# Moving the query preparation of the next tile behind the head loop, and two int8 steps from VectorE to GpSimd, in a two-layer attention/FFN kernel

## The reference, cut to what matters

```python
# x: (8, 4096, 1024) float32, one batch element per core
x = x + ln(attn(ln(x), gamma0, w_qkv0, w_out0))     # layer 0, attention
x = x + ln(int8_ffn(ln(x), rhs))                    # layer 0, FFN with absmax int8
x = x + ln(attn(ln(x), gamma1, w_qkv1, w_out1))     # layer 1, attention
x = x + ln(qlora_ffn(ln(x), ...))                   # layer 1, six 4-bit linears with LoRA

# attn: 8 heads of 128, causal; l2-normalised rows, qkv, softmax(q k^T) v, out projection
# int8_ffn: s = max(|x|)/127 per row; q = round(x/s); (q @ q_rhs) * s * s_rhs
```

## Time and profile before

| | us |
|---|---|
| median of 3 runs | 8509.21 |
| lowest and highest | 8452.44, 8510.84 |
| the profiled execution | 8492.97 |
| its span, first to last instruction (core 1) | 8491.4 |
| TensorE busy | 4956.7 (58%) |
| VectorE busy | 2899.7 (34%) |
| ScalarE busy | 3002.4 (35%) |
| GpSimd busy | 481.8 (6%) |
| mean granted TensorE clock | 0.764 of full |

### The profile page before, as it was taken

How to read it: one execution, slowest core, us unless ns; L and a number is a source line. 1 busy time by engine, 2 the same in 40 slices (tenths; PEclk the granted TensorE clock), 3 DMA queues, 4 the chain that set the end, 5 groups by cost and what they waited for, 6 DMA issues and landing times.

```text
span 8491.4 us, 56576 instructions; the slowest of 8 cores (8444.4 to 8491.4 us)
## 1 busy us (share of the span) xinstructions
PE 4956.7 (58%) x18624; PEld 1752.6 (21%) x18624; DVE 2899.7 (34%) x4937; ACT 3002.4 (35%) x4569; POOL 481.8 (6%) x612
## 2 busy tenths in 40 slices
PE   4644566677679333366455667677780566667553
PEld 1221111122122111122111122222220222222121
DVE  4443322221221566444333221221213433433445
ACT  1212334344457121122123344445551243333332
POOL 0001000000000000000000000000002101100000
PEclk8766778788789666666667788788895787778776
DMA  2021101000100121300211100000004201110111
GB/s 75 30 65 44 36 28 35 33 29 19 33 25 9 63 89 72 109 30 30 66 40 40 36 29 23 33 29 18 25 19 140 70 1 41 41 33 13 52 47 57
DMA packets 120312, 362.13 MB, mean 43 GB/s; under 512 B 24464, under 2 KB 24464, under 8 KB 120016
## 3 DMA queue, kind: packets, MB, share of 16 engines
q1 hardware_dynamic: 120016, 358.51, 13.0%
HBM read 291.07 MB, written 67.37 MB: 42 GB/s over the span
## 4 chain that ended last, share of the span: by engine, by line
PE 50%; DVE 22%; DMA 14%; ACT 8%; issue 3%; POOL 2%; SPq 1%; DVEq 0%; ACTq 0%
PE pf L813 8%; PE pf L853 8%; PE pf L1136 8%; PE pf L842 7%; DMA xq<-xbuf 4%; PE pf L638 3%; PE pf L912 3%; ACT probs L823 3%; DVE rcp_row L864 3%; PE pf L664 3%; PE pf L742 2%; DMA xq<-x 2%; PE pb L481 2%; POOL probs L831 2%; DMA xbuf<-xq 2%
## 5 line engine op out<-in xcount | busy, mean ns | idle before, releaser
L823 ACT ACTIVATE probs<-pf,negM_col 128x512 bf16<-128x512 f32 x2304 | 1582.8, 687 | 1495.9 <-PE pf L813 1480.6
L481 PE MATMUL pb<-ident_bf,prep_bf 128*128 128x128 bf16 x1536 | 198.6, 311 | 1710.2 <-DVE prep_bf L723 705.6
L842 PE MATMUL pf<-probs,v_sb 128*128 128x512 bf16 x2304 | 946.4, 411 | 415.2 <-ACT probs L823 236.5
L864 DVE RECIPROCAL rcp_row<-pf 1x512 f32<-1x512 f32 x128 | 428.3, 3346 | 2005.2 <-PE pf L853 2004.7
L813 PE MATMUL pf<-qT,kT 128*128 128x512 bf16 x2304 | 951.4, 422 | 16.3 <-ACT qT L747 16.3
L853 PE MATMUL pf<-probs,ones_col 128*1 128x512 bf16 x2304 | 915.3, 397 | 0.0
L831 POOL TENSOR_SCALAR_AFFINE_SELECT probs<-probs 128x512 bf16<-128x512 bf16 x512 | 313.4, 612 | 6006.6 <-ACT probs L823 6006.6
L481 PEld LDWEIGHTS pb<-ident_bf,prep_bf 128*128 128x128 bf16 x1536 | 148.0, 141 | 1768.0 <-DVE prep_bf L723 725.5
L1148 ACT ACTIVATE ySB<-pf,bcol 128x512 bf16<-128x512 f32 x384 | 263.8, 687 | 694.4 <-PE pf L1140 690.5
L540 ACT ACTIVATE sq<-pb 128x1024 bf16<-128x1024 bf16 x128 | 131.0, 1023 | 913.1 <-DVE cols L534 913.1
L1136 PE MATMUL pf<-hT,wbuf 128*128 128x512 bf16 x1536 | 386.3, 397 | 50.2 <-ACT ySB L1148 47.5
(11 more groups left out here) (134 smaller groups left out, 5346.3 us busy)
## 6 DMA issues: line engine op xcount, KB each, us to landing
xq<-xbuf SPq DMA_DIRECT2D x128, 512.0 KB, 3.5
xbuf<-xq SPq DMA_DIRECT2D x96, 512.0 KB, 2.6
xq<-x SPq DMA_DIRECT2D x64, 512.0 KB, 4.6
rcp_bc<-rowrt SPq DMA_DIRECT2D x128, 256.0 KB, 3.7
xq4f<-xbuf SPq DMA_DIRECT2D x64, 512.0 KB, 4.0
wstage<-wqkvT SPq DMA_DIRECT2D x48, 512.0 KB, 4.4
wstage_i<-qwT SPq DMA_DIRECT2D x48, 512.0 KB, 3.7
screp<-scT SPq DMA_DIRECT2D x384, 64.0 KB, 2.3
```

What stands on the lines that cost most here:

```text
L481: v = p.add("tensor", lambda e, j=j: e.transpose(M.pb[pslot][:, j, :], M.prep_bf[:, prep_slot, j * 128:(j + 1) * 128], M.ident_bf[:]), wai ...
L823: ev = p.add("scalar", lambda e, kc=kc, h=h, ps=ps: e.activation(M.probs[:, kc % 2, :], ps[:], AF.Exp, bias=M.negM_col[:, h:h + 1], scale= ...
L842: p.add("tensor", lambda e, h=h, kc=kc, pO=pO: e.matmul(pO[:], M.v_sb[:, kc, h * 128:(h + 1) * 128], M.probs[:, kc % 2, :], start=(kc == 0 ...
L864: rc = p.add("vector", lambda e, pR=pR: e.reciprocal(M.rcp_row[:], pR[0:1, :]), waits=rw, inc="ve")
```

## The change

Two parts. In attention, `q_prep_tile` and `q_mm_group` go back into `q_prep` and `q_mm`. The head loop holds no preparation. After the last head the four row tiles are prepared, then the out projection runs, then all eight groups of Q, then `bound_prep` and the epilogue as before. In the int8 FFN, scaling and rounding go to GpSimd, in place in one of two buffers (`apply_scr`, `scrF2`), and the two casts, the transposes and the copy of row tile i are emitted by `_quant_fin` after the normalisation and the scale steps of row tile i+1. The casts wait for GpSimd.

```diff
@@ emit_prologue_group, mode "quant"
+    qpend = []
+    def _quant_fin(t, i, rne, B):
+        p.add("vector", lambda e, B=B: e.tensor_copy(M.scrI[:], B[:]),
+              waits=[("ge", rne)], inc="ve")
+        ps_ = i % 2
+        gw2 = [p.prep_gate[ps_]] if p.prep_gate[ps_] else []
+        vap = p.add("vector", lambda e, ps_=ps_: e.tensor_copy(
+            M.prep_bf[:, ps_, :], M.scrI[:]), waits=gw2, inc="ve")
+        consume(t, i, ("ve", vap), i % 2)
...
+            B = (M.apply_scr, M.scrF2)[i % 2]
...
-            zv = p.add("vector", lambda e, t=t: e.tensor_scalar(
-                M.apply_scr[:], M.apply_scr[:], cf[:, t, 2:3], None, ALU.mult),
-            p.add("vector", lambda e: e.tensor_scalar(
-                M.apply_scr[:], M.apply_scr[:], MAGIC, -MAGIC, ALU.add, ALU.add),
-                inc="ve")
-            p.add("vector", lambda e: e.tensor_copy(M.scrI[:], M.apply_scr[:]),
-                  inc="ve")
+            p.add("gpsimd", lambda e, t=t, B=B: e.tensor_scalar(
+                B[:], B[:], cf[:, t, 2:3], None, ALU.mult),
+                waits=[("ve", cv)], inc="ge")
+            rne = p.add("gpsimd", lambda e, B=B: e.tensor_scalar(
+                B[:], B[:], MAGIC, -MAGIC, ALU.add, ALU.add), inc="ge")
+            p.f0chain_gate[i % 2] = ("ge", rne)
+            qpend.append((t, i, rne, B))
+            if len(qpend) > 1:
+                _quant_fin(*qpend.pop(0))
+    while qpend:
+        _quant_fin(*qpend.pop(0))
@@ emit_attn, end of the head loop
-            if qt + 1 < nq:
-                if h == 0:
-                    qp_evs = []
-                if h < 4:
-                    q_prep_tile(qt + 1, h, qp_evs)
-                    if h == 3:
-                        xnT_ready = ("ve", max(qp_evs))
-                else:
-                    qev_n = q_mm_group(h - 5, xnT_ready) if h >= 5 else None
         attnout_ready = ("ve", p.c("ve"))
-        p.feat8_gate = None
+        if qt + 1 < nq:
+            xnT_ready = q_prep(qt + 1)
@@ after the out projection
         if qt + 1 < nq:
-            for fo in range(3, H):
-                qev_n = q_mm_group(fo, xnT_ready)
-            p.xnT_free[0] = p.add("scalar", _nop, inc="nf0")
-            qT_ready = ("ae", qev_n)
+            qT_ready = q_mm(qt + 1, xnT_ready)
             negM_evs = bound_prep(qt + 1, qT_ready)
```

More of the change, by code:

```diff
@@ L60, in __init__ @@
         self.rows_gate = []
-        self.f0chain_gate = None
+        self.f0chain_gate = [None, None]
         self.negMb_gate = [None] * 8
@@ L349, in emit_prologue_group @@
             p.xq_free[bufs[i][2]] = p.c(bufs[i][2])
+            consume(t, i, ("ve", vap), i % 2)
         else:
+            B = (M.apply_scr, M.scrF2)[i % 2]
             p.add("vector", lambda e, t=t, sve=sve: e.reciprocal(cf[:, t, 1:2], sve),
                   waits=[("ae", sq)], inc="ve")
-            aw2 = [p.f0chain_gate] if p.f0chain_gate else []
-            p.add("vector", lambda e, t=t, xsl=xs[i]: e.tensor_scalar(
-                M.apply_scr[:], xsl, cf[:, t, 0:1], cf[:, t, 1:2], ALU.add,
+            aw2 = [p.f0chain_gate[i % 2]] if p.f0chain_gate[i % 2] else []
@@ L356, in emit_prologue_group @@
+            p.add("vector", lambda e, t=t, xsl=xs[i], B=B: e.tensor_scalar(
+                B[:], xsl, cf[:, t, 0:1], cf[:, t, 1:2], ALU.add,
                 ALU.mult), waits=aw2, inc=["ve", bufs[i][2]])
             p.xq_free[bufs[i][2]] = p.c(bufs[i][2])
-            p.add("vector", lambda e: e.tensor_reduce(
-                col(M, 8), M.apply_scr[:], AX.X, ALU.max,
+            p.add("vector", lambda e, B=B, i=i: e.tensor_reduce(
+                col(M, 8 + i % 2), B[:], AX.X, ALU.max,
                 apply_absolute_value=True), inc="ve")
-            p.add("vector", lambda e: e.tensor_scalar(col(M, 9), col(M, 8), 1e-12,
-                                                      1.0 / 127.0, ALU.max,
-                                                      ALU.mult), inc="ve")
@@ L364, in emit_prologue_group @@
-            p.add("vector", lambda e, t=t: e.reciprocal(cf[:, t, 2:3], col(M, 9)),
-                  inc="ve")
[L366 to L369, removed]
-            zv = p.add("vector", lambda e, t=t: e.tensor_scalar(
-                M.apply_scr[:], M.apply_scr[:], cf[:, t, 2:3], None, ALU.mult),
-                inc="ve")
@@ L382, in emit_prologue_group @@
-        consume(t, i, ("ve", vap), i % 2)
+            p.add("vector", lambda e, i=i: e.tensor_scalar(
+                col(M, 10 + i % 2), col(M, 8 + i % 2), 1e-12,
+                1.0 / 127.0, ALU.max, ALU.mult), inc="ve")
+            p.add("vector", lambda e, t=t, i=i: e.reciprocal(
+                cf[:, t, 2:3], col(M, 10 + i % 2)), inc="ve")
+            p.add("vector", lambda e, t=t, i=i: e.tensor_mul(
+                col(M, 12 + i % 2), cf[:, t, 2:3], cf[:, t, 2:3]), inc="ve")
+            cv = p.add("vector", lambda e, t=t, i=i: e.tensor_scalar(
+                cf[:, t, 3:4], col(M, 12 + i % 2), 1e-5, None, ALU.mult),
+                inc="ve")
@@ L383, in emit_prologue_group @@
+    if mode == "quant":
+        return None
     return None
@@ L705, in emit_attn, with q_prep @@
     nq = min(NQ, LIMIT_BQ)
-    def q_prep_tile(qt, tt, evs):
-        for tt in (tt,):
+    def q_prep(qt):
+        evs = []
+        for tt in range(4):
             t = qt * 4 + tt
@@ L728, in q_prep_tile @@
             evs.append(emit_prep_to_xnT(p, M, tt, 0, tp))
[L730 to L733, removed]
         return ("ve", max(evs))
[L736 to L750, removed]
     def q_mm(qt, xnT_ready):
         for fo in range(H):
-            qev = q_mm_group(fo, xnT_ready)
+            pfk = M.pf[fo % 2]
+            w0 = [xnT_ready, wq_ready]
+            if p.pf_gate[fo % 2]:
+                w0.append(p.pf_gate[fo % 2])
+            for fi in range(NF):
+                mv = p.add("tensor", lambda e, fo=fo, fi=fi, pfk=pfk: e.matmul(
+                    pfk[:], M.wbuf1[:, fi, fo * 128:(fo + 1) * 128],
+                    M.xnT[:, 0, fi, :], start=(fi == 0), stop=(fi == NF - 1)),
+                    waits=(w0 if fi == 0 else ()),
+                    inc=("mm" if fi == NF - 1 else None))
+            qev = p.add("scalar", lambda e, fo=fo, pfk=pfk: e.activation(
+                M.qT[:, fo, :], pfk[:], AF.Copy), waits=[("mm", mv)], inc="ae")
+            p.pf_gate[fo % 2] = ("ae", qev)
         p.xnT_free[0] = p.add("scalar", _nop, inc="nf0")
@@ L893, in emit_attn @@
             p.pO_gate[hp] = ("ve", nv)
-            if qt + 1 < nq:
-                if h == 0:
-                    qp_evs = []
-                if h < 4:
-                    q_prep_tile(qt + 1, h, qp_evs)
-                    if h == 3:
-                        xnT_ready = ("ve", max(qp_evs))
-                else:
-                    qev_n = q_mm_group(h - 5, xnT_ready) if h >= 5 else None
+        p.feat8_gate = None
         attnout_ready = ("ve", p.c("ve"))
-        p.feat8_gate = None
+        if qt + 1 < nq:
+            xnT_ready = q_prep(qt + 1)
         for oc in range(NF):
```

## The result

The changed kernel takes 7965.68 us (median of 9 runs, 7897.94 to 8013.29) against 8501.17 us for the kernel before (median of 10). The ratio is 0.9377, with a 95% interval of 0.9338 to 0.9416: 6.2% faster. The forecast was 7920 us, range 7840 to 7990, so the time fell inside it. In some executions the cores of one die, or of both, show a lower granted TensorE clock and take longer; the ratios leave these executions out, and where a profiled execution was one of them (gpsimd_mult_add) its rows are read on core 1, on the undisturbed die. From profiled execution to profiled execution the span fell by 532 us, from 8491.4 to 7959.2, where the sum of the prediction had 589.

A forecast was written before the change was run, and what follows sets the result against it. No engine was near its limit, so waits set the time, chiefly TensorE's for `prep_bf`. 8493.0 - 569 (796 less 227) - 20 = 7904 us profiled; the median is 16 us above, so 7920 us, range 7840 to 7990.

The forecast's parts named there:

- The stall and its size: Attention head loop: stalls at preparations behind heads' tails, and Q groups after heads 5 and 6, go; 796 us less.
- The new end of a tile: After a query tile's last head: four preparations delay the out projection, more Q groups follow; 16.2 us per tile, 227 us.
- Part 2: Int8 FFN: moving scaling and rounding from VectorE to GpSimd gains 20 us.
- the wait for GpSimd is about nothing: Int8 FFN: GpSimd's two steps take 2.1 to 3.1 us, which other VectorE work fills.
- The collision term: Int8 FFN: one VectorE instruction per row tile is stretched by 0.87 us beside GpSimd, cutting the gain from 48 to 20.
- Rival A: Int8 FFN: both GpSimd steps are slow and collide, -35 us instead of +20; 7975 us, 18 in 100.
- B: New `q_prep`: the third and fourth x loads are not hidden, at most 139 us; 8060 us, 5 in 100.
- C: Short query tiles: TensorE stays at its lower clock level, 334 us; 8255 us, 3 in 100.
- D: Head loop: the wait moves to the matmuls with V instead of going; slower, 8716 us, 2 in 100.
- The sum: Whole kernel: 8493.0 us profiled less 569 for attention and 20 for the int8 FFN, 7904 us.

The follow-up runs named there:

- gpsimd_mult_add: The changed kernel with its int8 rounding on GpSimd written as two multiply-adds instead of one add-add; 7973.43 us, ratio 0.9402.
- Experiment 6: The kernel before with the preparation after heads 0 to 3 moved ahead of that head's reciprocal, transfers and multiply; 7793.57 us, ratio 0.9228.
- experiment 1: The changed kernel's attention with the int8 FFN of the kernel before; 7931.02 us, ratio 0.9345.
- experiment 3: The kernel before with GpSimd instructions of several forms, 128x1024, added ahead of the int8 FFN; alone, add-add took 3.63 us, multiply-add 1.04.
- experiment 7: Experiment 6's kernel with Q groups 0 to 4 moved behind the last head and 5 to 7 behind the out projection; 7745.25 us, ratio 0.9048.

## Why the prediction came out as it did, point by point

**The stall and its size**: right. 796 us were to go and 787 went. Free heads run at 23.9 us in tile 5, 13.1 in tile 2, 9.5 in tile 1 and 8.6 in tile 0, against 23.8, 13.0, 9.4 and 8.65. Experiment 6 shows the cause: the same work ahead of the tail costs almost nothing.

**The new end of a tile**: right in its parts, 16 us low in this execution; in experiment 1, with the same code, the ends grew by 218 us, 9 less than the 227. The out projection starts 20.8 us after the last reciprocal on average, not 20.2. L897 of head 7 starts 9.5 us after it on average over tiles 1 to 6, and there the tails with one x load behind them had 8.5 before, and those of heads 4 to 6 in the changed kernel, with none behind them, 7.8. Now two loads follow at once; that they slow the broadcast load is inferred from these three numbers. The 10.03 us from the reciprocal to the first L723, read at one head, hid part of this: the 56 preparations before had 9.7 on average, and the 14 first ones after have 10.9. The four preparations took 9.9 us from the first L739 to the start of the out projection, as `q_prep(0)` said. From there to the first L782 33.4 us pass, 27.5 before; the term of the sum was 5.3, measured 5.9 here and 4.0 in experiment 1. That it differs between the two is the granted clock.

**Part 2** is the step that failed, on its sign: +27 us for -20, of which 24 are clear of noise. The term was GpSimd's duration. It was taken from L1062 as "the nearest row: a tensor_scalar of the same size", and size was the wrong likeness. The row is a multiply-add with two constants; the new steps are a multiply by a column and an add-add, at 2.9 and 3.6 us alone (experiment 3). With them "the wait for GpSimd is about nothing" falls as well. The timeline of VectorE after, in the group of row tiles shown above, has the casts of the first, second and last of the four. VectorE waits 2.4 us at the first and 3.1 us at the last, and not at the second:

```profile
2720.59 0.69 DVE L319 CAST scrI<-apply_scr 128x1024 int32<-128x1024 f32 x1 [2.44 <-POOL apply_scr L388]
...
2727.86 0.69 DVE L319 CAST scrI<-scrF 128x1024 int32<-128x1024 f32 x1
2728.58 1.49 DVE L323 CAST prep_bf<-scrI 128x1024 bf16<-128x1024 int32 x1
...
2742.29 0.69 DVE L319 CAST scrI<-scrF 128x1024 int32<-128x1024 f32 x1 [3.13 <-POOL scrF L388]
```

In between a row tile takes 7.2 to 7.3 us, as the prediction had it, and neither engine waits for the other by more than 0.2 us: GpSimd's 7.2 us are as long as VectorE's chain of a row tile, its wait for the transposes included. So the loss is at the ends of the groups. The waits there come to 5.6 us a group, 45 us in eight, which is about what VectorE was relieved of (48), and the held-up instructions come on top. The collision term was right in size: one instruction per row tile is held up, three of the four casts of a group by 0.7 to 0.8 us (1.41 to 1.49 for 0.69) and its second normalisation by 0.7 (1.52 for 0.81), where 0.87 was taken. The rule of the Trainium skill that the prediction weighed (SBUF — State Buffer, "Who interferes with whom") holds in its direction only: by it the later one waits for the whole instruction of the other, but the cast of 2728.58 ended at 2730.07, while GpSimd's L385, which had started at 2727.90 and took 3.38 us (in the chain above), was still running. Rival A described this outcome, at -35 us, with 18 in 100. Its mechanism, waits at the first and last row tile of a group because GpSimd's steps are slow, is what the trace shows: 45 us of such waits for its 27, with 7.0 us of GpSimd's work per row tile for its 4.7, and one collision for its two. Its reason was not: it went by float32 operands, and experiment 3 has the multiply-add from float32 at 1.04 us.

**The rivals B, C, D**: none occurred. Four preparations took what `q_prep(0)` took (B); the heads of the short tiles ran at the free period (C); and the wait moved only where the prediction already had the tail chain as the period (D). TensorE's waits after have this row, all of it in tile 0 of the two layers, against the 227 us from which D would decide:

```profile
PE pf L849 <- DVE feat L897: 19.9, 8, 3.1
```

**The sum**: 532 us measured for 589 in the profiled execution. Of the 57 us missing, 47 are part 2, 16 the ends, 9 the heads, less 15 in stretches of unchanged code. These 15 us are luck, and without them the median would still lie within the range. The range held although part 2 had the wrong sign, because part 2 was small beside part 1 and the range was drawn to take in rival A.

## What to carry to other kernels

An interleaved piece of work must stand in every engine's queue ahead of the slow chain that it is meant to hide, not behind it: in tile 5 the same instructions cost 13 us per boundary behind a head's tail, 0.1 us ahead of it, and 11.5 us per query tile when gathered at the end. In the two shortest tiles, whose heads are hardly longer than the tail, 2 to 3 us per boundary stayed. Taking work out of the loop cured the stall, but moving it up by one block cured it more cheaply, and left the tail free for five blocks of matmuls. Before an elementwise step is given to another engine, find the same operation on that engine in a trace, not just the same size, and look first whether the step is needed at all.

## What the runs showed of the hardware that was not expected

GpSimd's tensor_scalar over 128x1024 took 1.04 us as multiply-add with two constants, 2.85 us as a multiply by a column, and 3.63 us as add-add with two constants, with VectorE idle. The add-add took the same in place or not, and the multiply-add the same from float32 or from int32. VectorE took 0.75 us for the multiply by a column and 0.69 for the add-add. The Trainium skill (GPSIMD Engine Reference, section "Engine selection") calls one-input operations on GpSimd roughly line-rate. The multiply-add, at 1.04 us for 1024 elements in each partition, agrees with that; the two others, at 2.7 to 3.5 times as long, don't.

The granted TensorE clock over the same stretch of matmuls, after the same idle time, was 0.84 in one execution and 0.92 in another, which made 1.9 us of difference per tile between two kernels with the same attention code. Where TensorE had work in the stretch before it (experiment 7), the out projection and what follows were granted 0.98 on average.
